# Token mixing of units 6 and 7 in float16 parts, and an instruction order written anew, in a four-layer kernel on one Trainium2 core

## The reference

```python
x = x + s4_block(layernorm(x))      # gates i, f, o, s: x@W + b; scan h = f*h + i*s over tokens;
                                    # z = xn + o*h, layernorm of z with gamma and beta
x = x + ffn(layernorm(x))           # first token-mixing layer
x = x + attention(layernorm(x))     # 16 heads of 16, causal over all 4096 tokens
x = x + ffn(layernorm(x))           # last token-mixing layer, same weights

def ffn(x, W_r, W_k, W_v, mu_r, mu_k):
    x_prev = x shifted by one token
    xr = mu_r*x + (1-mu_r)*x_prev;  xk = mu_k*x + (1-mu_k)*x_prev
    r = sigmoid(xr @ W_r.T);  k = relu(xk @ W_k.T)**2
    return r * (k @ W_v.T)
```

## Time and profile before

| | |
|---|---|
| three runs | 1675.02, 1678.70, 1678.71 us (median 1678.7) |
| the profiled execution | 1679.5 us, of which the span of its instructions is 1677.8 us |
| instructions | 50396 |
| mean granted TensorE clock | 0.994 of full |
| last reduce of maxima ends | 1579.8 us from the span's start |
| last exponential ends | about 1646.4 us |

### The profile page before, as it was taken

The page is one execution under the profiler, slowest core; times in us unless marked ns, Lnnn a source line. Parts: engine busy times, 40 slices in busy tenths (PEclk is TensorE's granted clock), DMA queues, the critical chain, the costliest instruction groups (busy, mean ns, idle before and its releaser), DMA issues.

```text
span 1677.8 us, 50396 instructions
## 1 busy us (share of the span) xinstructions
PE 1625.4 (97%) x20458; PEld 663.6 (40%) x20458; DVE 1511.0 (90%) x2905; ACT 1308.5 (78%) x2590; POOL 940.3 (56%) x1295
## 2 busy tenths in 40 slices
PE   8999999999999999999999999999999999999997
PEld 6656444444434344343443332333333332332214
DVE  6868998988999999999999999999999999999603
ACT  2535587667778877888878888988888999888994
POOL 3358878897995798768584534553523520425101
PEclk9999999999999999999999999999999999999999
DMA  4143223113122121131130110103110000000000
GB/s 110 46 90 59 50 56 61 47 42 63 46 45 52 33 52 31 28 57 40 31 59 10 27 33 8 32 19 66 20 25 9 25 8 20 15 14 15 9 1 14
DMA packets 127767, 61.59 MB, mean 37 GB/s; under 512 B 78512, under 2 KB 127536, under 8 KB 127536
## 3 DMA queue, kind: packets, MB, share of 16 engines
q1 hardware_dynamic: 125296, 57.33, 15.7%
q10 hardware_dynamic: 2240, 1.05, 0.4%
HBM read 25.31 MB, written 16.52 MB: 25 GB/s over the span
## 4 chain that ended last, share of the span: by engine, by line
PE 46%; DVE 41%; ACT 5%; POOL 4%; issue 4%; DMA 1%; ACTq 0%; POOLq 0%; DVEq 0%
DVE span_max L2088 34%; PE psum L2442 13%; PE psum L2397 8%; PE psum L2421 8%; PE psum L2168 4%; PE psum L2178 4%; PE psum L2149 3%; PE psum L2157 2%; ACT probs L1744 2%; DVE span_max L2082 1%; ACT probs L1733 1%; DVE small L1930 1%; DVE rows L2020 1%; PE psum L2451 1%; PE psum L2404 1%
## 5 line engine op out<-in xcount | busy, mean ns | idle before, releaser
L2088 DVE TENSOR_REDUCE span_max<-psum 128x1 f32<-128x512 f32 (+1 forms) x2048 | 1237.0, 672 | 35.1 <-PE psum L2397 28.1
L1733 ACT ACTIVATE probs<-psum 128x512 f32<-128x512 f32 (+3 forms) x1788 | 881.1, 568 | 173.0 <-PE psum L2421 169.7
L2397 PE MATMUL psum<-k_stack,q_stack 48*128 48x512 f16 (+3 forms) x2304 | 570.8, 364 | 8.8 <-DVE span_max L2088 5.3
L2421 PE MATMUL psum<-q_stack,k_stack 50*128 50x512 f16 (+3 forms) x2304 | 542.5, 364 | 8.9 <-ACT probs L1744 2.5
L2442 PE MATMUL psum<-probs,v_aug 128*17 128x512 f32 (+3 forms) x3968 | 486.1, 562 | 5.2 <-POOL probs L1569 3.8
L2421 PEld LDWEIGHTS psum<-q_stack,k_stack 50*128 50x128 f16 x2304 | 149.1, 93 | 399.9 <-ACT probs L1733 222.6
L2397 PEld LDWEIGHTS psum<-k_stack,q_stack 48*128 48x128 f16 x2304 | 168.7, 93 | 250.1 <-DVE span_max L2088 165.3
L1569 POOL TENSOR_SCALAR_AFFINE_SELECT probs<-probs 128x512 f32<-128x512 f32 x116 | 74.3, 644 | 182.5 <-ACT probs L1744 115.1
L1733 ACT ACTIVATE w_gates<-psum 128x512 f32<-128x512 f32 (+1 forms) x254 | 130.7, 573 | 17.0 <-PE psum L2421 16.8
L2442 PEld LDWEIGHTS psum<-probs,v_aug 128*17 128x17 f32 x3968 | 67.9, 95 | 119.5 <-issue 96.7
L1562 POOL TENSOR_TENSOR rows<-rows 128x512 f32<-128x512 f32 x26 | 33.2, 1275 | 141.0 <-ACT rows L1674 141.0
(11 more groups left out here) (242 smaller groups left out, 1905.3 us busy)
## 6 DMA issues: line engine op xcount, KB each, us to landing
q_stack<-q_parts SPq DMA_DIRECT2D x192, 32.0 KB, 2.0
k_stack<-k_parts SPq DMA_DIRECT2D x42, 128.0 KB, 4.8
rows<-in_x SPq DMA_DIRECT2D x16, 256.0 KB, 2.9
q_parts<-rows SPq DMA_DIRECT2D x32, 128.0 KB, 1.9
k_parts<-rows SPq DMA_DIRECT2D x32, 128.0 KB, 2.0
out<-rows SPq DMA_DIRECT2D x16, 256.0 KB, 2.3
x_rows<-rows SPq DMA_DIRECT2D x14, 256.0 KB, 2.6
rows<-x_rows SPq DMA_DIRECT2D x14, 256.0 KB, 2.7
```

The costliest lines, as they stand in the source:

```text
L1733: act.activation(probs_of(tile)[:, i, q0:], bank(b)[:, q0:], ACT.Exp, scale=SCALE / QK_SCALE).then_inc(exp_done, 1)
L2088: nc.vector.tensor_reduce(span_max[:, s % SPAN_RING, row:row + 1, k0 // SPAN:k0 // SPAN + 1], bank(b)[:, 0:k1 - k0], AX.X, ALU.max).then_i ...
L2397: ins = nc.tensor.matmul(bank(b)[:, at:at + k1 - k0], q_stack[row:row + SCORE_ROWS, s % Q_RING, v, qt * P:(qt + 1) * P], k_stack[row:row + ...
L2421: nc.tensor.matmul(bank(b)[:, q0:], k_stack[row:row + STACK, g * PAIRS + u, j * P:(j + 1) * P], q_stack[row:row + STACK, s % Q_RING, u, q0 ...
```

## The change

Two things change. The first mixing layer of units 6 and 7 is in float16 parts too. And the order of all queues is a new one: `schedule()` has the same code, but another `WORTH` in all 19 rows, DVE costs nearer to what the instructions take, and other landing times. One semaphore, `raw_scaled`, takes the place of two, and the transposes and stores of the maxima count on one semaphore per buffer in place of a shared one, with the same waits in meaning.

```diff
-TURNED_FROM = {FIRST: 8, LAST: 2}
+TURNED_FROM = {FIRST: 6, LAST: 2}
...
-WORTH = {"max": (310.80492, 3407.35767, 530.833233, 3336.0769, 3121.61172, 3238.82237, 2288.92567, 3874.75678,
+WORTH = {"max": (-675.700339, 3243.9693, 3419.0322, 3403.45362, 3121.61172, 3502.86666, 3969.75242, 3399.20303,
...
-            "r*kv": 605, "q.part1": 790, "kk.part1": 790, "x3": 600, "neg": 175, "part0": 90, "part1": 195,
+            "r*kv": 605, "q.part1": 790, "kk.part1": 790, "x3": 600, "neg": 175, "part0": 260, "part1": 300,
...
-            "bo.add": 338, "apply": 652, "z.apply": 1710, "subtract": 606, "accumulate": 610},
+            "bo.add": 338, "apply": 770, "z.apply": 1850, "subtract": 880, "accumulate": 850},
...
-           "load_x2": 500, "store_out": 500, "shift.turn": 1300, "shift.spill": 400, "place": 900}}
+           "load_x2": 500, "store_out": 500, "shift.turn": 1150, "shift.spill": 400, "place": 700}}
...
-         "load_q": 2400, "load_x2": 2700, "store_out": 2200, "shift.turn": 1300, "shift.spill": 1900, "place": 2200}
+         "load_q": 2400, "load_x2": 2700, "store_out": 2200, "shift.turn": 1500, "shift.spill": 1300, "place": 1400}
...
-LANDS_AT = {("store_x2", 1): 5500, ("store_x2", 2): 6500, ("x1.turn", 4): 5200, ("load_q", 0): 3600, ("load_q", 1): 3600}
+LANDS_AT = {("store_x2", 1): 3500, ("store_x2", 2): 4000, ("x1.turn", 4): 4000, ("load_x", 5): 5500, ("load_x", 6): 3500,
+            ("load_q", 0): 6500, ("load_q", 1): 5500, ("load_q", 2): 3800, ("shift.turn", 1): 3500}
...
-                        sp.wait_ge(spilled_shift, 16 * (s - 1))
+                        sp.wait_ge(spilled_shift[s % 2], 16 * (s // 2))
...
-                                           in_=shift_parts[:, s % 2, :]).then_inc(turned_shift, 16)
+                                           in_=shift_parts[:, s % 2, :]).then_inc(turned_shift[s % 2], 16)
...
-                            pe.wait_ge(ao_scaled, 1)
+                            pe.wait_ge(raw_scaled, 2)
```

More of the change, by code:

```diff
@@ new lines @@
+WORTH = {"max": (-675.700339, 3243.9693, 3419.0322, 3403.45362, 3121.61172, 3502.86666, 3969.75242, 3399.20303,
[3 rows of a table added]
+         "dve": (-0.709482114, 4.11763307, 1.92992508, 2.83468729, 3.00215546, 1.38627325, 3.18211868, 4.99011869,
[3 rows of a table added]
+         "scores": (-1385.77109, 1871.25299, 2441.08163, 1986.98636, 1982.56483, 1526.94071, 530.531935, 966.412804,
+            2588.5378, 2055.77499, 1904.37144, 2489.09124, 2664.48383, 2588.5378, 1724.33285, 1106.51635, 2588.5378,
+            2664.48383, 2603.80208, 1729.8973, 2025.87462, 1053.75348, 2664.48383, 530.531935, 1620.50451,
+            1685.44345, 1042.19244, 2877.34266, 1620.50451, 442.857356, 2664.48383, 1323.69),
+         "act": (1.44525, 1.68998276, 1.1390755, 1.79022375, 1.78271425, 1.55207256, 1.97122623, 2.01669927,
[3 rows of a table added]
+         "half": (-859.142091, 1168.67286, -2571.66346, -2017.14697, -1197.75565, 7314.67622, 11867.6423, 5324.99996,
[7 rows of a table added]
+         "stay": (557.733789, 12075.106, -2959.92473, 4347.23511, 10956.0568, -4975.73538, 4746.48419, 10937.4824,
[3 rows of a table added]
+         "two": (10838.2942, -2375.72708, -345.644552, 25977.9468, 11934.205, 6348.63193, 16958.0837, -2942.41707,
[3 rows of a table added]
+         "ring": (-118.757835, 1769.91775, -27.727296, -1774.39709, 861.949088, 298.240806, -8249.32492, 600.575322,
[3 rows of a table added]
+         "last": (4459.46217, -1433.20254, 836.977715, 2684.39999, 1111.31722, 1125.58774, 1218.34739, 429.845149,
[3 rows of a table added]
+         "job": (1632.91368, 1010.68105, 1512.97304, 1319.41141, 1556.85572, 1713.43734, 1634.08766, 3340.54057,
[3 rows of a table added]
+         "age": (0.0351727006, -0.0667460646, -0.0177473304, -0.0354360992, -0.0357931749, -0.00523947632,
+            -0.118153798, -0.0452332102, 0.00672432308, -0.063301481, 0.0188822483, -0.0825318917, -0.0850367855,
+            0.00522219294, -0.0335494521, -0.211201544, 0.00522219294, -0.0277475406, -0.0041659785, 0.0130602877,
+            -0.0338857184, -0.0970680372, -0.0271032898, -0.118153798, -0.593775997, -0.335865257, -0.406213884,
+            0.0281026188, -0.704504857, -0.409262733, -0.0230852582, -0.435398),
+         "same": (69993.9409, 2622.43021, 13479.4968, -77401.4476, -77401.4476, 2180.66106, 19711.5147, 16843.3568,
[3 rows of a table added]
+         "after": (-412.221234, -467.59011, 237.073723, -228.901671, -509.028642, 188.670747, 631.623263, 645.700733,
[3 rows of a table added]
+         "rest": (8871.12506, 533.17501, -15578.0045, -899.423463, -815.592147, -14081.795, 4444.09266, -24521.3961,
[3 rows of a table added]
+         "free": (413.300562, -181.651523, 380.973812, -120.138213, -132.970448, 211.118907, 731.404628, 380.973812,
[3 rows of a table added]
+         "more": (208.476338, -625.708954, -176.229259, -537.72946, -601.090534, -651.237406, -624.296719,
[3 rows of a table added]
@@ L208 @@
             -861.634),
-         "queue": (-129.035252, 139.911085, 616.630434, -483.946534, -234.234954, -480.060377, 442.102773,
[3 rows of a table removed]
+         "queue": (-669.346597, -211.004241, -196.222084, -290.166875, 3923.36658, -115.628776, -6.80779589,
[3 rows of a table added]
             -1868.04),
-         "stock": (177.996176, 64.9651376, -5.04777574, 15.9477195, -39.2145812, 16.1741038, -21.6600092, 59.8559768,
[3 rows of a table removed]
+         "stock": (129.528908, 131.131826, 115.526245, 45.0305688, -32.1834041, 127.533633, 76.474523, 30.3748788,
[3 rows of a table added]
@@ L1010, in build @@
             sem(n) for n in ("squared", "sums_read", "clipped", "powered", "w_scaled", "w_qk_scaled", "w_hi", "w_lo"))
-        a_lo, a_turned, ao_loaded, ao_scaled = (sem(n) for n in ("a_lo", "a_turned", "ao_loaded", "ao_scaled"))
+        a_lo, a_turned, ao_loaded = (sem(n) for n in ("a_lo", "a_turned", "ao_loaded"))
         hi_ready = sem("hi_ready")
@@ L1050, in build @@
         span_reduced = sem("span_reduced")
-        neg_ready, part_ready, shift_ready, turned_shift, spilled_shift = (
-            sem(n) for n in ("neg_ready", "part_ready", "shift_ready", "turned_shift", "spilled_shift"))
+        neg_ready, part_ready, shift_ready = (sem(n) for n in ("neg_ready", "part_ready", "shift_ready"))
+        turned_shift, spilled_shift = ([sem(f"{n}_shift{b}") for b in range(2)] for n in ("turned", "spilled"))
         shift_placed = [sem(f"shift_placed{b}") for b in range(2)]
```

45 lines of the change are left out of this document (10 added, 35 removed), and 101 rows, old and new, of the table WORTH.

## The result

The changed kernel takes 1681.2 us (median of 20 runs, 1679.3 to 1686.0), the kernel before 1677.4 (20 runs beside them): a ratio of 1.0025, interval 1.0018 to 1.0033. I had forecast 1673.2. The time is inside the range of 1663 to 1685, but above the 1679 at which I had called the forecast wrong, and the direction is wrong. The difference of 3.8 us is just under what I had called the limit of telling; with 20 runs of each kernel its interval stays clear of no change.

A forecast was written before the change was run, and what follows sets the result against it. Time was taken as DVE's work plus 82.8 us idle to the last reduce, ACT's 67 us, then a closing chain; only idle and ACT's stretch could change. 1679.5 - 3.3 - 2.0 + 4.0 - 3.9 - 1.1 = 1673.2 us, range 1663 to 1685.

The forecast's parts named there:

- The mixing on PE, -3.3: Units 6 and 7: faster float16 jobs and dropped float32 transposes save PE 3.3 us, counted whole as time.
- Fewer changes of tiling, -2.0: PE's order has 31 fewer tiling changes at 0.13 us, 4.0 us; half counted, -2.0.
- work given back, -3.9: Scores and pv that PE does during DVE's stand at chunk 3 spare later DVE idle: -3.9 us.
- POOL, +4.0 at the start of chunk 3: More POOL work makes unit 7's keys 4.0 us later; DVE stands 4.0 us at chunk 3's start.
- in the ends above: Queues standing for a too short landing time got no term, only the terms' low and high ends.
- The end, -1.1: Behind the last reduce, 70 double and 11 single exponentials in place of 76 and 2: -1.1 us.
- The base: Starting time of the sum: profiled execution of the kernel before, 1679.5 us, 0.8 above the three runs' median of 1678.7.
- Rival 1: PE's saving hidden and chunk 3's stand given back; DVE and POOL set the pace: 1678.4 us, chance 0.25.
- Rival 2: Keys of units 6 and 7 late, chunk 3 starts 11.6 us late, mark 385.2 us: 1688.0 us, chance 0.12.
- Rival 3: POOL slows DVE: six scans of units 7 to 9 wait 1.16 us each, +7.0: 1680.2 us, chance 0.05.
- Rival 4: New order gains more: DVE's idle behind 480 us halves, 9.5 us more: 1663.7 us, chance 0.15.

The follow-up runs named there:

- less work on PE, in before: Kernel before, with 6 of 8 matmuls kept in the 12 product jobs of units 6 and 7's first mixing layers: 1676.9 beside 1677.1 us, 1.0002.
- y first: Changed kernel, with POOL's product making y of unit 10 moved ahead of unit 2's residual and the sum of unit 8's turned parts: 1677.1 us, 1.0004.
- the splices: PE's order joined at maximum 396 in step 18: changed kernel's (y of unit 10 moved ahead) then before's, 1686.8 us; before's then changed kernel's, 1686.9 us.
- the form alone: Kernel before, its PE and mixing-layer order and tables kept, with units 6 and 7's first mixing layers in the new float16 form: 1707.3 us, 1.0193.
- keys later, less work: Changed kernel, y of unit 10 moved ahead, chunk 6's keys loaded one place later, two of three partial products in 12 jobs: 1680.1 us, 1.0010.
- less work on POOL: Changed kernel, with eight low parts of units 6 and 7's first mixing layers written as zeros, 4.3 us less on GpSimd: 1680.9 us, 1.0027.
- second splice: Kernel before up to maximum 396 in step 18, then the changed kernel's order, no layer in the new form: 1686.9 us, 1.0067.

## Why the prediction was wrong, point by point

- **The mixing on PE, -3.3, "taken whole": the step that failed.** The saving is real: PE's groups of the float32 products shrink by 8.8 and 5.3 us, its transposes to channels by 1.7, and the float16 groups grow by 10.3, so 5.5 us in all, more than the 3.3 I had. But as time it is worth 0 in the order of before, where that question can be put alone (less work on PE, in before: 1.0002, steps 8 to 11 within 0.3 us), and leaving more away in the new order cost 6 to 7 us. I took DVE's wait at 265.85 as proof that PE's length sets the pace there. It showed that DVE waited for PE, not that everything behind it would come sooner if PE's jobs were shorter: the keys of unit 7 were stored no earlier. Which wait took up the 2.6 us isn't settled. In the changed kernel steps 8 to 11 are 3.7 us longer, not 3.3 shorter.
- **Fewer changes of tiling, -2.0, and work given back, -3.9.** Both needed the same pace. DVE's idle behind chunk 3's start was to fall to 17 us; it is 29.8, and 24.5 (10.4 and 14.1) with y first. Steps 12 to 17 take 0.5 us more than in before although y costs 4 of them; steps 18 to 31 take 3.8 us more (3.2 with y first), so here the new order loses nearly as much as at y. Of these 3.8 us 2.4 are DVE's work that came earlier in before, 1.5 idle. Why isn't settled, since the splices brought waits of their own.
- **POOL, +4.0 at the start of chunk 3.** The price was right by luck, and the reason wrong. The keys of unit 7 are stored at 386.5, 7.9 us later, inside the 4 to 10 I gave; but in the eight other profiles that share this order up to there they are stored at 387.1 to 391.3, six of them over 10 us later. No cost of it shows: 4.3 us less of POOL's work changed nothing that can be told, and with y first, the keys stored at 391.3, PE waits for no keys; it stands 0.93 us before the first maximum, 0.1 us behind the landing of a load of queries. DVE's two waits there still come to 4.4 us; but for those 0.93 it is PE's own order that makes them. What cost 4 us was one wait for a DMA, in a queue, ahead of one operation that was ready. I had written that the queues would stand if a landing time was too short and put it "in the ends above"; it deserved a place. The table has 2.7 us for the load of the residual; behind six loads of keys it took 6.5.
- **The end, -1.1:** 96.6 us behind the last reduce for 97.9, as forecast.
- **The chain of the new form, which I left at nothing.** I counted its POOL work but not that its products come 7 to 11 us later. In the new order PE doesn't wait for these parts, so no term shows it; the form alone shows its price in the old one.
- **The base.** The three runs shown had their median 1.3 us above that of 20, the profiled one 2.1.
- **The rivals.** Rival 1 (hidden) describes the kernel with y first, 1.0004, in its number: the lengths of the steps differ both ways. Rival 2's sign came true and its mark was passed (386.5 beyond 385.2, DVE's two waits 9.0 us where it wanted over 8), without its mechanism. Rival 3 fell: the scans became shorter, not longer.

```profile
L2021 DVE TENSOR_TENSOR_SCAN rows<-rows,small x8: 724/1029/1583, 257.8 to 396.8; 128x256 f32<-128x256 f32 x8
```

The median between 200 and 400 us is 1029 ns against 1515, beside more work of POOL, since the order put them at other moments: of the eight, the two at 396 us have no instruction of POOL beside them and take 0.73 us, the six that have one take 0.94 to 1.58. The rule of the Trainium skill that I had weighed ("SBUF — State Buffer", "SBUF: two separate sides") is about what runs at the same instant; the total of GpSimd's work says nothing about that here. Rival 4 fell.

In sum: 1677.4 as base, nothing for PE, nothing that can be told for POOL's work, +4.2 for y in its queue, -1.3 for the end. That makes 1680.3 for 1681.2 and looks complete, but part of it is luck: besides y, steps 8 to 11 take 3.7 us more, 12 to 17 3.5 less and 18 to 31 3.8 more. The first seven steps must have given the rest back, and there profiles scatter too far to tell.

## What to carry to other kernels

In an order written out for engines that each take their queue in turn, saved work is worth what the next wait leaves of it, and that can be nothing; before counting a saving, look for the wait that comes second. Look at each wait for a DMA on a queue for what stands behind it and is ready: moving one such operation ahead paid 3 to 4 us in both kernels, as much as I had forecast for the form. And a change that lengthens a chain and tables fitted to the program are one change: neither can be priced, or tried, without the other. Compare two traces by the lengths of their steps, not by moments: a length that repeats within 0.1 us shows a place worth 1 us where whole runs scatter by 6 or 7.

## What was unexpected

- **A stand of 2.5 to 3 us cost 3.4 to 4.7.** Waits of PE of 0.7 and 1.1 us left the clock whole. Of the longer ones, 1.75 (keys later, less work) and 2.5 us (less work on POOL) were followed by 3.4 us at the lower clock, 2.8 and 3.0 us by 6.8, and one of 3.4 (second splice) by 3.4 again (0.54 granted in 940 to 945 us, a job of 24 matmuls 1.47 us instead of 0.84); the 2.45 us for the mask in before were followed by none. The steps show the price: 4.0 us less for the stand of 2.8 taken away, 4.7 more for one of 3.0 in place of 0.7, 3.4 less for the one of 2.45 (where before has 3.4 us at the lower clock in the same step, ahead of the stand).
- **Turns by DMA are slow beside a large load, and beside a load of instructions.** A pair of turns landed after 2.5 us alone, 4.2 behind six loads of 128 KB, and 5.8 with a transfer of 16 KB of instructions besides. In the profile with y first I took all turns of rows behind 600 us that had no other load or store in flight: the 37 without a transfer of instructions between issue and landing took 2.39 to 2.54 us, the 11 with one up to 4.15.
- **Less work can cost time.** 2.7 us of TensorE's work left out made the kernel 6 to 7 us slower, 4.7 of them in one step 500 us later, where transfers of instructions now fell upon the turns. With 96 matmuls fewer these transfers came 2.2 us earlier against the order's own work, and the tables of the scheduler have no row for them.
